# A Mamba and attention block on one NeuronCore: SiLUs, narrow copies, squares and an output sum change places, and the MLP's narrow input stays in PSUM

## The reference, cut to what matters

```python
# layer 0, for one image; xn = rmsnorm(x)
u, z  = split(xn @ in_proj_w.T)
for flow in (forward, backward):
    uc    = silu(conv4(u) + conv1d_b)
    dt, B, C = split(uc @ x_proj_w.T)              # 24 + 16 + 16 columns
    delta = softplus(dt @ dt_proj_w.T + dt_proj_b)
    h[n]  = exp(delta * A[n]) * h[n] + delta * uc * B[n]     # 16 states n, along 1024 tokens
    y     = sum_n C[n] * h[n] + uc * D_param
    out  += (y * silu(z)) @ out_proj_w.T
x = x + res_scale * (scale_mod * out + sigmoid(conv3x3(xn) + dw_b) * xn)
# layer 1
t = t + attention(layernorm(t))        # causal, 6 heads of 64
t = t + gelu(layernorm(t) @ kron(c_fc_1, c_fc_2).T) @ kron(c_proj_1, c_proj_2).T
```

## Time and profile before

| | us |
|---|---|
| median of three runs | 4040.74 |
| the profiled execution, its own time | 4045.01 |
| its span | 4043.1 |
| VectorE busy | 3526.4 (87%) |
| TensorE busy | 3405.5 (84%) |
| GpSimd busy | 2820.7 (70%) |
| ScalarE busy | 2593.5 (64%) |

### The profile page before, as it was taken

One profiled execution on the slowest core, in us unless ns is written; L12 is line 12 of the kernel. 1 busy time (PEld: TensorE's weight loads), 2 busy tenths in 40 slices (PEclk: granted clock), 3 DMA queues, 4 the chain that ended last, 5 costly groups with the idle time before them and its releaser, 6 DMA issues.

```text
span 4043.1 us, 39821 instructions
## 1 busy us (share of the span) xinstructions
PE 3405.5 (84%) x11722; PEld 1723.8 (43%) x11722; DVE 3526.4 (87%) x2678; ACT 2593.5 (64%) x3592; POOL 2820.7 (70%) x1714
## 2 busy tenths in 40 slices
PE   7504499989999898988899889988989889985999
PEld 2101136623474245723366234742457233651473
DVE  6999999999999999999999999999999999999121
ACT  4533567676686767756676756867677666766363
POOL 3889886687866877677866878668776778668000
PEclk8757699988999899988999889988999889997999
DMA  3999897898977998788987989788987889789000
GB/s 103 234 248 240 190 242 181 207 209 207 219 190 188 227 214 202 190 201 198 237 188 199 222 202 216 186 193 224 215 198 194 203 201 232 179 197 221 6 7 16
DMA packets 220548, 770.79 MB, mean 191 GB/s; under 512 B 24908, under 2 KB 40574, under 8 KB 220062
## 3 DMA queue, kind: packets, MB, share of 16 engines
q0 software_dynamic: 113616, 413.71, 52.9%
q1 hardware_dynamic: 106702, 354.32, 26.4%
HBM read 339.60 MB, written 39.85 MB: 94 GB/s over the span
## 4 chain that ended last, share of the span: by engine, by line
PE 43%; DVE 21%; issue 12%; ACT 9%; POOL 8%; DMA 7%; ACTq 0%; DVEq 0%; POOLq 0%
DVE pB L1313 14%; PE pW L710 9%; PE pW L623 9%; DMA y<-hb 6%; PE pW L511 6%; POOL hb L1527 5%; PE pW L588 3%; PE pW L639 3%; PE pW L554 3%; ACT pt L1071 2%; POOL prob L1501 2%; PE pW L785 2%; DVE hb L1322 1%; PE pW L602 1%; PE pW L742 1%
## 5 line engine op out<-in xcount | busy, mean ns | idle before, releaser
L1313 DVE TENSOR_TENSOR_SCAN pB<-pB,hb 128x1024 f32<-128x1024 f32 x768 | 1757.4, 2288 | 64.1 <-ACT pB L889 52.1
L1542 POOL DMA_DIRECT2D y<-hb x765 | 748.9, 979 | 628.0 <-DVE hb L1322 578.3
L1527 POOL TENSOR_TENSOR hb<-du_f,b_row 128x1024 f32<-128x1024 f32 x384 | 1003.3, 2616 | 157.4 <-DMA y<-hb 71.9
L1527 POOL TENSOR_TENSOR hb<-uc_b,b_row 128x1024 f32<-128x1024 f32 x384 | 996.4, 2596 | 75.2 <-DMA y<-hb 62.0
L1322 DVE TENSOR_TENSOR hb<-pB,c_row 128x1024 f32<-128x1024 f32 x768 | 940.5, 1225 | 44.6 <-DVE pB L1313 0.5
L889 ACT ACTIVATE pB<-delta,vec 128x1024 f32<-128x1024 f32 x384 | 429.2, 1118 | 303.2 <-DVE hb L1322 290.3
L889 ACT ACTIVATE pB<-xres,vec 128x1024 f32<-128x1024 f32 x384 | 427.9, 1119 | 214.7 <-DVE hb L1322 213.7
L710 PE MATMUL pW<-area,pt 128*128 128x64 f32 x3456 | 440.1, 282 | 19.2 <-ACT pt L1071 11.5
L710 PEld LDWEIGHTS pW<-area,pt 128*128 128x128 f32 x3456 | 413.1, 196 | 68.9 <-ACT pt L1071 58.8
L1360 DVE TENSOR_REDUCE stat<-pW 128x1 f32<-128x640 f32 (+7 forms) x361 | 258.7, 753 | 162.4 <-PE pW L626 162.4
L530 PE MATMUL pW<-area,xn_area 128*128 128x512 f32 x576 | 260.7, 608 | 31.9 <-DVE area L1418 19.0
(11 more groups left out here) (185 smaller groups left out, 5010.3 us busy)
## 6 DMA issues: line engine op xcount, KB each, us to landing
y<-hb POOLq DMA_DIRECT2D x765, 512.0 KB, 7.7
b_row<-bc_rows SPq DMA_DIRECT2D x256, 512.0 KB, 5.9
c_row<-bc_rows SPq DMA_DIRECT2D x256, 512.0 KB, 5.8
du_f<-in_x SPq DMA_DIRECT2D x8, 1536.0 KB, 13.9
kept_residual<-in_x SPq DMA_DIRECT2D x8, 1536.0 KB, 18.9
xres<-kept_residual SPq DMA_DIRECT2D x8, 1536.0 KB, 14.5
out_x<-xa SPq DMA_DIRECT2D x7, 1536.0 KB, 9.5
kept_residual<-hb POOLq DMA_DIRECT2D x16, 512.0 KB, 5.3
```

What stands on the lines that cost most here:

```text
L1313: dve.tensor_tensor_scan(flow(d, buf), flow(d, buf), flow(d, hb[r % NHB][:, :]), 0.0, ALU.mult, ALU.add).then_inc(scan_done, 1)
L1527: pool.tensor_tensor(hb[r % NHB][:, :], du[d][:, k, :], b_row[g % 2][:, :], ALU.mult)\
L1542: pool.dma_start(y[:, k, :], hb[r % NHB][:, :], accum_op=ALU.add).then_inc(y_in[k], 16)
```

## The change

Seven edits, none of which alters a result beyond rounding. (1) `mlp_add` is one row later (82 and 92 instead of 81 and 91). (2) `wo_add` 5 comes behind `next_norm` in row 66. (3) `next_square` comes behind decay(64) instead of ahead of it. (4) `step_silu` joins SOON, so in row 17 the SiLUs come ahead of the copy of `proj` 2. (5) The narrow input is scaled into PSUM (`pS`, banks 0 and 1 of `pW`) and its casts and subtractions read and write it there. (6) The copy of 32 partitions from VectorE (L1404) becomes a second ScalarE copy out of PSUM behind `mlp_low`. (7) In the head, the narrow copies come ahead of tap 8, the first sigmoid and the table load, and the first softplus step ahead of the second sigmoid.

```diff
-        ("mlp", c * (NFG + 1) + NFG, r + 2 * NFG), ("mlp_out", c, r + 2 * NFG), ("mlp_add", c, r + 2 * NFG + 1)]
+        ("mlp", c * (NFG + 1) + NFG, r + 2 * NFG), ("mlp_out", c, r + 2 * NFG), ("mlp_add", c, r + 2 * NFG + 2)]
...
-    + [("wo_add", t, S1 + (3 if t < 2 else 5)) for t in range(6)]
-    + [("next_square", 0, S1 + 2), ("next_mean", 0, S1 + 2), ("next_rstd", 0, S1 + 4), ("next_norm", 0, S1 + 5)]
+    + [("wo_add", t, S1 + (3 if t < 2 else 5)) for t in range(5)]
+    + [("next_square", 0, S1 + 2), ("next_mean", 0, S1 + 2), ("next_rstd", 0, S1 + 4), ("next_norm", 0, S1 + 5), ("wo_add", 5, S1 + 5)]
...
-SOON = [x for x in BEHIND if x[0] == "step_abs"]
+SOON = [x for x in BEHIND if x[0] in ("step_silu", "step_abs")]
...
                 elif kind == "mlp_cast" and early and not alone(b):
                     act.wait_ge(xr_scaled, at(2, a, 2))
-                    act.copy(xr_a, xr_rest[:, :]).then_inc(xr_step, 1)
+                    act.copy(xr_a, pS).then_inc(xr_step, 1)
                 elif kind == "mlp_low" and early and not alone(b):
                     act.wait_ge(xr_step, at(5, a, 2))
-                    act.copy(xr_b, xr_rest[:, :]).then_inc(xr_step, 1)
+                    act.copy(xr_b, pS).then_inc(xr_step, 1)
+                    act.copy(xr_a[3 * KI:4 * KI, :], pS[3 * KI:4 * KI, :]).then_inc(xr_step, 1)
...
-                elif kind == "next_square" and early:
+                elif kind == "next_square" and not early:
...
-                    tap_row_of(b, TAPS[6], 9)
+                    tap_row_of(b, TAPS[6], 8)
+                    narrow_copies(b, 0)
+                    tap_row_of(b, 8, 9)
                     gates(b, 0, 1)
-                    narrow_copies(b, 0)
-                    gates(b, 1, 2)
                     soft_abs(b, 0, 0)
-                    gates(b, 2, 3)
+                    gates(b, 1, 3)
...
-                        dve.tensor_tensor(part, part, pW[:, c, :], ALU.mult).then_inc(xr_scaled, 1)
+                        dve.tensor_tensor(pW[:, c, :], part, pW[:, c, :], ALU.mult).then_inc(xr_scaled, 1)
                 elif kind == "mlp_split" and not early and not alone(b):
                     dve.wait_ge(xr_step, at(5, a, 1))
-                    dve.tensor_tensor(xr_rest[:, :], xr_rest[:, :], xr_a, ALU.subtract).then_inc(xr_step, 1)
+                    dve.tensor_tensor(pS, pS, xr_a, ALU.subtract).then_inc(xr_step, 1)
                 elif kind == "mlp_fix" and not early and not alone(b):
                     dve.wait_ge(xr_step, at(5, a, 3))
-                    dve.tensor_copy(xr_a[3 * KI:4 * KI, :], xr_b[3 * KI:4 * KI, :]).then_inc(xr_step, 1)
-                    dve.tensor_tensor(xr_b[0:KI, :], xr_rest[0:KI, :], xr_b[0:KI, :], ALU.subtract)\
+                    dve.tensor_tensor(xr_b[0:KI, :], pS[0:KI, :], xr_b[0:KI, :], ALU.subtract)\
```

More of the change, by code:

```diff
@@ L1156, in iteration @@
                         act.preload_act_table_set(LOG_EXP)
-                        item("next_square", 0, -1, True)
+                        item("next_square", 0, -1, False)
                         prepare()
```

## The result

The changed kernel takes 4057.49 us (median of six runs, 4053.26 to 4062.08) against 4043.52 for the kernel before beside it (4040.47 to 4049.57): a ratio of 1.0036, with a 95% interval of 1.0025 to 1.0047. It is slower by 14 us, outside the forecast range of 4016 to 4052. Its profiled execution has a span of 4051.3 and an own time of 4053.26, both 8.2 above those of before. No trace shows the other 6.

A forecast was written before the change was run, and what follows sets the result against it. VectorE, busy 87% of the span, and TensorE, 84%, were both taken as near the bound. Terms 22 + 7 - 19 - 5 - 7 - 2.6 = -4.6 us took the median from 4040.7 to 4036, range 4016 to 4052.

The forecast's parts named there:

- Row 17: SiLUs first: projection 4 waits for projection 2's bank and holds `step_x`, so scan 22 comes later; +22 us, bounds +15 and +28.
- Rows 63 to 71: Squares behind decay(64) bring scan 64 2.0 sooner, but `next_norm` meets GpSimd and scan 71 comes 1.7 later; +7 us.
- The collision with GpSimd: Row 66: `next_norm`, starting at 1266.0, meets a GpSimd product begun at 1265.77; 2.1 us added.
- Rows 71 to 76: One 32x1024 subtraction with a PSUM input replaces L1404 and L1405 in row 72; -19 us, bounds -24 and -12.
- The stall of 1.0 at scan 75: Scan 75 waits 1.0 us on the ScalarE path through `mlp` 0, GELU and decay(75), leaving 2.5 gained in six images.
- `mlp_add`: One row later, scan 83 loses its stall but decay(85) stays where it is; 0.7 gained in each of seven images, -5 us.
- The head with row 92: New head order, row 92 inside it, brings the first sum sooner, -7 us; image 7 keeps row 92's stall as gain, -2.6.
- S: End of TensorE's `step_x` in the head, 1403.97 in head 2; first sum forecast at S + 12.5, before at S + 13.7.
- (b): Rival: as forecast, but no collision in row 66, late heads early, TensorE's clock kept up; -21 us, 4020; 26%.
- (a): Rival: TensorE does not push back, so each stall seen on VectorE goes; -85 us, 3956; 5%.
- (c): Rival: `step_x` isn't held, so moving the SiLUs first costs nothing; 4014; 7%.
- (d): Rival: DMAs into `y` land late in five heads, first tap of channel tile 2 waiting over 2.5 us; +11, 4051; 17%.

The follow-up runs named there:

- five filling matmuls: Changed kernel plus five further 128x512 matmuls on TensorE ahead of projection 4 in row 17, filling its idle time: 4052.21 us, ratio 1.0014.

## Why the prediction was wrong, step by step

**Row 17 (+22 recorded, +30.4 measured).** The mechanism was right in each link: `step_x` behind `proj` 4, `proj` 5's copy waiting for TensorE, decay(22) late. Undoing edit 4 takes all 30 back. The term that was mis-sized is "takes 2.6 (a tile of six instructions is 10.46 / 4)". That row came from a TensorE that had just been busy. Here it had been idle for 5.29. The two stretches below are the first 2 us of `proj` 4 in images 2 and 4 (length, busy us of PE, PEld, DVE, ACT, POOL, PEclk, DMA share, GB/s):

```profile
1036.48:1038.50 2.02, 2.02 (x3) 0.98 (x4) 1.03 (x1) 2.02 (x3) 2.02 (x2) 0.50 1.01 340
1976.43:1978.50 2.07, 2.07 (x5) 1.06 (x6) 1.08 (x1) 2.07 (x3) 2.07 (x2) 1.00 1.01 339
```

In image 2 the granted clock is at its lower level, 1.2 GHz, and the tile takes 4.35. In image 4 it idled 3.59, the clock stayed at the upper level, and the tile took 2.84:

```profile
1976.43 2.84 PE L511 MATMUL pW<-xn_area,w_qp 128*128 128x512 f32 x6 [3.59 <-ACT area L1049]
```

There row 21 stalls for 4.3, near the recorded 3 to 4; elsewhere for 5.7 to 6.9. Over the seven images `proj` 4 took 30.9 where the recorded sum had 7 x 2.6 = 18.2; of the 12.7 more, 8.4 are left in rows 17 to 31. The five filling matmuls put it to the test: with the upper clock back `proj` 4 took 19.4 in all, and row 21 stalled for 3.6 to 5.5.

**Rows 63 to 71 (+7 recorded, +22.9 measured).** This is the step that failed. "Moved sooner by 2.0, it waits for tile 4 instead, and `next_norm` starts at 1266.0" is false: `next_norm` begins with a wait of its own,

```python
                elif kind == "next_norm" and not early:
                    dve.wait_ge(wo_ready, at(6, b, 0))
```

and 6b finished tiles are all six of image b - 1. The norm writes where the `wo` products read, so the wait is real. I read the instructions of the item and not its waits. The 2 us of the squares therefore end in row 66, and nothing is left to set against what I had seen rightly but put too low: TensorE's second half of `ln_mean` held by `wo_add` 5 (2.33 in image 2 and 22.2 in images 1 to 6 together, no gap before), the narrow input late (19.5 us at L1399). The collision with GpSimd that I had put at 2.1 came in images 3, 4 and 5 (in image 3 it had been there before), smaller in 1 and 6, not in 2. All norms together took 39.2 instead of 34.0. These are the times of L1418 (min/median/max):

```profile
L1418 DVE SCALAR_TENSOR_TENSOR area<-du_f,vec,prob x24: 1214/1276/3361, 20.7 to 3163.9; 128x1024 f32<-128x1024 f32 x24
```

Undoing edit 2 gives 20 (with edit 4 in) and 23 (without); undoing edit 3 as well, another 1 to 4 by the rows.

**Rows 71 to 76 (-19 recorded, -24.5 measured).** L1405 takes 1202 ns, as forecast, and row 72 is 3.5 shorter in each of seven images. Before, L1405 had begun 0.43 us ahead of a GpSimd product of 2.64 and ended 1.1 behind it, in all seven; now that product begins 1.0 after L1405 does and overlaps it for 0.2. How much of the gain is the operand's in PSUM and how much that of the other place in time, no run separates. The stall of 1.0 at scan 75 was too large: 0.2 in images 1 to 6, since `mlp` 0's six matmuls followed each other every 0.32 us there and took 2.0. The 2.9 was what they had taken in image 2 before, where the granted clock was 0.62 on average while they ran; now it was 1.00. Of the operands in PSUM the trace shows next to nothing: `mlp_split` takes 1222 ns where it took 1216, `mlp_scale` 696 where it took 682. By the Trainium skill, "VectorE: DVE Perf Modes", section "The TRN2 errata", a read from PSUM would cost 62 cycles more, an estimated 0.06 us. `mlp_split`, which now reads PSUM in the place of SBUF, shows 0.006, and the measurement decides; `mlp_scale` read PSUM before as well, and its 0.014 came with writing there.

**`mlp_add` (-5 recorded, -1.3 measured in the profile).** Row 82's stall went in all seven images (0.9 to 2.6, 10 in all). Row 84 got one, 0.3 or 1.9 to 2.0, 8.6 in all, as "decay(85) stays where it is" has it. Beside the kernel that differs in this edit alone it is worth 4.7 and 6.3 in these rows, so the term was sound.

**The head with row 92 (-9.6 recorded, -22.4 measured).** From S the sum was right: first sum at S + 12.5 recorded, S + 12.48 in four of seven heads, S + 11.84 to 11.99 in three where TensorE's first step size was done sooner (from S + 2.2 its four matmuls took 2.0 to 2.5 instead of 3.8; this is rival (b)'s half microsecond). In the head behind image 5 it was, too, but there `local` took 3.45 and the sum came at S + 12.47. What I held fixed was S itself. It came 80.3 behind scan 79 on average before and 78.6 after, 7 x 1.8 = 12 us sooner. In the eleven other profiles of kernels with four or more of the edits it lies between 78.9 and 79.5, so about a third of that is this one execution's. It does not hang on edit 7 (79.5 with it undone) or on edit 1 (79.3 and 79.1), and what moves it stays open. A part of it may be in how the convolution ran: its first 32 instructions took 14.0 us in some heads and 15.5 to 17.0 in others, after idle times of 0 to 2.0 that no releaser explains.

**The rivals.** (a) and (b) are out by the result, and (c) since `step_x` started 6.3 behind the SiLUs' end in image 2. (d) was seen in its mechanism, not in its price: the first tap waited for the DMA into `y` in the heads behind images 1, 2, 4 and 6 (2.62, 1.68, 0.54 and 2.78; before, in two heads, 1.88 and 2.17). Two of these are over the 2.5 that was to decide for it. Behind images 1 and 6 TensorE then stood idle for 2.19 and 1.80 until a SiLU behind the taps was done, so (d) ate a part of the gain; from row 86 on these two images took 73.1 instead of 74.4 and 72.1 instead of 75.7 all the same. The slower result is none of the rivals; it is the forecast with two losses put too small, by 8 and 16, against gains put too small by 5 and 13, a term that gave 4 less in this profile and 3 in rows that were put at nothing: from -4.6 to +8.2. The rest of the miss is the last step of the sum, which took the profiled execution to lie 4.3 above the median of its kernel; for the changed kernel it lay 4.2 below. That 8.5 says nothing of the kernel. That the head gained 13 more than recorded covered as much of the loss, and was luck: S had been held fixed without a reason given.

## What to carry to other kernels

When an item is moved ahead of a wait, read the waits that the item itself begins with: if it needs the same producer, the move gains nothing and delays whatever stood behind it. When a step leaves an engine's queue idle for some microseconds, price what follows on TensorE at its lower clock as well, and look for a row at that level. A change made of several edits is worth taking apart: here two edits cost 56 us by the medians and the others saved 42, and the whole looked like a small loss.

## What was not expected of the hardware

After idle times of 5.29 and 2.90 us TensorE began at a granted clock of 0.50, after one of 3.59 it kept 1.00 (images 2, 5 and 4 of the changed kernel): the length of the idle time alone does not tell. A 128x512 f32 matmul is recorded as two instructions and takes 0.87 us. A VectorE subtraction that reads and writes PSUM in the place of SBUF was 6 ns longer, a product that writes PSUM 14 ns. The subtraction that had taken 4160 ns beside a GpSimd product, with both inputs in SBUF, took 1202 to 1203 in all seven images with one of them in PSUM and another place in time.
